# First cross attention of a six-stage decoder: one element deeper in flight, keys masked on ScalarE

## The chip, the cores and the metric

The kernel runs on one core of one Trainium2 chip, as one launch. The metric is the device time of that core in microseconds (us); before the change it was 3356.13, the median of three runs from 3353.65 to 3359.01.

## What is computed

Two decoder layers over 64 elements of 128 tokens with 128 features, all in float32. Each of six parts adds its result to x and normalises: a gated linear attention, **a cross attention with 16 heads of 8 features**, a mixture of experts, a selective scan, a second cross attention with 16 heads of 64 features, and a feed-forward with ternary weights. The change touches the first cross attention alone:

```python
qh = (q @ Wq + bq).reshape(b, n, HEADS, DK).transpose(0, 2, 1, 3)      # b = 64, n = 128, HEADS = 16, DK = 8
kh = (k @ Wk + bk).reshape(b, -1, HEADS, DK).transpose(0, 2, 1, 3)     # k = v = ctx_1024, 77 rows
vh = (v @ Wv + bv).reshape(b, -1, HEADS, DK).transpose(0, 2, 1, 3)
scores = jnp.einsum('bhnd,bhmd->bhnm', qh * scale, kh)
scores = scores + attn_bias[:, None, :, :] + attention_mask[:, None, :, :]
probs = jax.nn.softmax(scores, axis=-1)
ctx = jnp.einsum('bhnm,bhmd->bhnd', probs, vh)
ctx = ctx.transpose(0, 2, 1, 3).reshape(b, n, HEADS * DK)
return ctx @ Wo + bo
```

Around it stands `x = _layernorm(x + _L0_xattn_ref(x, ctx_1024, ctx_1024, fside_BxSxS2_0, mask_BxSxS2_ff0, ...))`.

## The kernel before

`build` (end of the file) runs the parts as phases one behind the other: `run_phase` calls the phase and then `finish_statistics`, and each phase opens and closes its semaphores with blocks of all engines. x stays in SBUF for the whole kernel. The first cross attention is `phase_cross0` (L574 to L918); its names begin with `b_`.

Its unit of work is one batch element `i` of 64. The 16 heads are four quads `r` of four heads `j`. A head has only 8 features, so four heads share a group of 32 rows of PE: `keys` (L778) writes the projected keys four times, each copy multiplied by `head_mask`, a mask with the softmax scale in it that leaves one head's 8 rows in every group of 32. `score` (L850) then needs four matmuls of 32 rows with 4 x 77 = 308 columns. `values` (L788) writes v four times in the same way, times `b_v_mask`, a mask of 77 x 512 that is loaded from memory, and `mix` (L876) multiplies the copy of head `j` with the transposed probabilities, four column groups at a time.

One element goes through these steps, each a small function of its engine's block, with a semaphore for each result:

- ACT `normalise` (L716, writes `b_xs`), PE `turn_x` (L836), ACT `copy_xT`, PE `project` (L842: q, k and v into one PSUM bank), ACT `copy_q`, DVE `keys`, DVE `values`, PE `score`;
- DVE `bias_max` (L794: adds the side input and takes the row maximum), POOL `lower` (L679: subtracts it), ACT `exp`, DVE `sums` (L806: sum and reciprocal), POOL `divide` (L685);
- PE `turn_p` and ACT `copy_p`, four times, once per `j`, with two PSUM banks in turn, PE `mix` behind each; ACT `copy_c`, PE `project_out` (L888), DVE `leave` (L812: adds to x and takes the statistics).

The order of the work is written out by hand: each engine has a function `step(i, s)` that says which stage of which element it does in step `i`, and the engines run their steps in order. In step `i` element `i` is turned and mixed, `bias_max`, `lower` and `exp` are done for element `i + 2`, `sums` and `divide` for `i + 1`, the scores on PE for `i + 3`, the projections, keys and values for `i + 4`, and ACT ends its step with `normalise(i + 5)`. Every buffer has four slots (`slots`, L579), so `values(i + 4)` has to wait for the last mix of element `i`. `turn_x` waits for `values` of the element ahead, since both use the bank `b_in_ps`. `around` (L645) writes the first ten and the last eight steps out and runs the 52 in between in a hardware loop, four steps a round:

```python
for i in range(-5, 5):
    step(i, i % slots)
with eng.Fori(5, B - 10, slots) as i:
    for k in range(slots):
        step(i + k, (1 + k) % slots)
for i in range(B - 7, B + 1):
    step(i, i % slots)
```

## Time and profile before

| what | us |
|---|---|
| median of three runs (lowest, highest) | 3356.13 (3353.65, 3359.01) |
| the profiled execution | 3354.66 |
| its span in the profile | 3352.8 |
| busy: PE, DVE, POOL, ACT | 2726.7, 2409.3, 2033.2, 1716.0 |
| first row of the phase on ACT, last on DVE | 184.26, 651.24 |

All other tables and rows of this document are from that one execution. Times in a timeline count from the span's start. The phase of the change lies between 184 and 651 us. `PE` is the matmul engine, `PEld` its loading of weights, `DVE` the vector engine, `ACT` the scalar engine, `POOL` GpSimd, `SP` the engine that starts the DMAs; L747 is line 747 of the kernel. A float32 matmul is recorded as two or more instructions. Matmuls overlap, so from one to the next it is the starts that count, and the same holds for instructions of ACT and DVE that follow without a wait.

### The profile page before, as it was taken

How to read it: one execution, taken by the hardware profiler on the slowest of the kernel's cores; microseconds unless marked ns; L12 is line 12 of the kernel's file. 1: busy time of each engine (PE TensorE's matmuls, PEld its weight loads, DVE VectorE, ACT ScalarE, POOL GpSimd, SP SyncE). 2: the span in 40 equal slices, each digit the busy share in tenths (PEclk: the TensorE clock that was granted, in tenths of full speed). 3: DMA queues.
4: the chain of work that ended last, by engine and by line, in shares of the span. 5: the costliest groups of instructions: out<-in, count | busy, mean ns of one | idle time of the engine just before them, and what ended most of it. 6: DMA issues, size and time to landing. Idle time of an engine off the chain costs nothing. (4 is left out here: it accounts for less than half of the span.)

```text
span 3352.8 us, 51512 instructions
## 1 busy us (share of the span) xinstructions
PE 2726.7 (81%) x16584; PEld 1624.9 (48%) x16584; DVE 2409.3 (72%) x3855; ACT 1716.0 (51%) x3206; POOL 2033.2 (61%) x1795
## 2 busy tenths in 40 slices
PE   7868888799788817888798788868999999997555
PEld 5545555455455512333333333325777777775222
DVE  6968888655433344999989999885666666665777
ACT  7746666533222205656566665534444444443665
POOL 5447777556545546999989999862333333333444
PEclk9979999889899958899988998889999999998555
DMA  6810000011044433334333333310000000000000
GB/s 208 334 21 18 17 18 16 4 34 38 32 140 137 126 107 139 139 140 151 131 147 139 141 151 128 149 63 16 5 3 5 5 3 5 5 3 1 13 16 22
DMA packets 130121, 249.21 MB, mean 74 GB/s; under 512 B 41057, under 2 KB 97910, under 8 KB 109314
## 3 DMA queue, kind: packets, MB, share of 16 engines
q1 hardware_dynamic: 119250, 228.98, 19.9%
q0 software_dynamic: 9088, 16.94, 1.5%
q8 instruction: 107, 1.75, 0.2%
q10 hardware_dynamic: 1584, 0.79, 0.1%
q14 instruction: 92, 0.75, 0.1%
HBM read 189.34 MB, written 59.13 MB: 74 GB/s over the span
## 5 line engine op out<-in xcount | busy, mean ns | idle before, releaser
L1819 POOL TENSOR_TENSOR s_drive<-s_du,s_b_sb 128x1024 f32<-128x1024 f32 x256 | 599.0, 2354 | 35.3 <-DVE s_state_ps L2066 34.8
L2179 PE MATMUL s_y_ps<-s_read,w_ident 128*128 128x512 f32 x832 | 451.6, 673 | 163.2 <-DVE s_read L2079 163.0
L2066 DVE TENSOR_TENSOR_SCAN s_state_ps<-s_decay_ps,s_drive 128x512 f32<-128x512 f32 x416 | 486.6, 1215 | 98.0 <-ACT s_decay_ps L1965 87.0
L1965 ACT ACTIVATE s_decay_ps<-s_delta,neg_rate 128x508 f32<-128x508 f32 x512 | 346.4, 685 | 316.0 <-DVE s_state_ps L2066 266.0
L2179 PEld LDWEIGHTS s_y_ps<-s_read,w_ident 128*128 128x128 f32 x832 | 158.6, 204 | 426.6 <-DVE s_read L2079 266.2
L2417 ACT ACTIVATE c_pT<-c_turn_ps 77x512 f32<-77x512 f32 x256 | 149.1, 587 | 244.8 <-PE c_turn_ps L2618 244.5
L2079 DVE TENSOR_TENSOR s_read<-s_state_ps,s_c_sb 128x1024 f32<-128x1024 f32 x208 | 254.7, 1224 | 7.2
L2373 POOL TENSOR_TENSOR c_p<-c_p,c_norm 128x1232 f32<-128x1232 f32 x64 | 143.8, 2247 | 156.5 <-DVE c_norm L2498 156.5
L1422 POOL DMA_INDIRECT m_y_scratch<-e_y,e_index x156 | 152.6, 978 | 134.5 <-DVE e_index L1456 59.9
L2351 POOL TENSOR_TENSOR x<-c_xs,w_c_bo 128x128 f32<-128x128 f32 x64 | 30.8, 482 | 304.6 <-DVE c_xs L2458 304.6
L747 ACT ACTIVATE b_pT<-b_turn_ps 77x512 f32<-77x512 f32 x256 | 145.5, 591 | 120.1 <-PE b_turn_ps L872 120.1
L681 POOL TENSOR_TENSOR b_p<-b_p,b_top 128x1232 f32<-128x1232 f32 x64 | 143.9, 2248 | 93.8 <-DVE b_top L804 93.8
L1046 POOL DMA_INDIRECT m_rows_scratch<-m_xs,m_index x128 | 126.2, 986 | 94.8 <-DVE m_xs L1174 54.7
L872 PE MATMUL b_turn_ps<-w_ident,b_p 128*77 128x128 f32 x1024 | 162.3, 293 | 15.2 <-POOL b_p L687 15.2
L687 POOL TENSOR_TENSOR b_p<-b_p,b_norm 128x1232 f32<-128x1232 f32 x64 | 143.9, 2248 | 29.4 <-DVE b_norm L810 29.3
L2618 PEld LDWEIGHTS c_turn_ps<-w_ident,c_p 128*77 128x77 f32 x1024 | 124.7, 150 | 73.2 <-issue 47.6
L2618 PE MATMUL c_turn_ps<-w_ident,c_p 128*77 128x128 f32 x1024 | 155.1, 280 | 4.5 <-POOL c_p L2373 3.5
L2475 DVE TENSOR_TENSOR c_v<-c_f_ps,w_c_bv 77x512 f32<-77x512 f32 x128 | 87.8, 686 | 95.9 <-PE c_f_ps L2588 95.9
L2425 ACT ACTIVATE c_oT<-c_f_ps 128x512 f32<-128x512 f32 x128 | 76.4, 597 | 152.2 <-PE c_f_ps L2636 152.2
L2480 DVE TENSOR_REDUCE c_top<-c_s_ps 128x16 f32<-128x1232 f32 x64 | 92.2, 1441 | 79.7 <-PE c_s_ps L2602 79.7
L2602 PEld LDWEIGHTS c_s_ps<-c_k,c_q 64*128 64x128 f32 x2048 | 119.3, 188 | 51.2 <-issue 51.2
L1441 ACT ACTIVATE e_silu<-e_g_ps 128x512 f32<-128x512 f32 x78 | 46.6, 598 | 190.6 <-PE e_u_ps L1497 155.5
(371 smaller groups left out, 6931.2 us busy)
## 6 DMA issues: line engine op xcount, KB each, us to landing
s_b_sb<-s_bc_scratch SPq DMA_DIRECT2D x64, 1024.0 KB, 4.7
s_c_sb<-s_bc_scratch SPq DMA_DIRECT2D x64, 1024.0 KB, 4.7
m_rows_scratch<-fill SPq DMA_DIRECT2D x33, 1040.0 KB, 27.5
e_w<-in_m_we_dram SPq DMA_DIRECT2D x39, 384.0 KB
e_xg<-m_rows_scratch SPq DMA_DIRECT2D x39, 260.0 KB
k_y<-m_y_scratch SPq DMA_DIRECT2D x32, 256.0 KB, 3.6
out_dram<-q_result SPq DMA_DIRECT2D x16, 256.0 KB, 2.3
x<-in_x_dram SPq DMA_DIRECT2D x13, 256.0 KB, 2.8
```

What stands on the lines that cost most here:

```text
L681: nc.gpsimd.tensor_tensor(p[:, s, :, :], p[:, s, :, :], top[:, s, :].unsqueeze(2).broadcast_to([128, heads, S2]), ALU.subtract).then_inc(l ...
L687: nc.gpsimd.tensor_tensor(p[:, s, :, :], p[:, s, :, :], norm[:, s, :].unsqueeze(2).broadcast_to([128, heads, S2]), ALU.mult).then_inc(p_no ...
L747: nc.scalar.activation(pT[:, j, :, :], turn_ps[0:S2, j % 2, :].rearrange("p (r t) -> p r t", t=128), ACT.Copy).then_inc(pT_ready.sem, 1)
L872: last = nc.tensor.transpose(turn_ps[0:S2, j % 2, r * 128:(r + 1) * 128], p[:, s, per * r + j, :], core.ident[:, :])
L1422: nc.gpsimd.indirect_dma_start(y_dram[:, :], bass.IndirectOffsetOnAxis(index[:, t % y_slots, j:j + 1], 0), y[:, t % y_slots, j, :], None, ...
L1819: nc.gpsimd.tensor_tensor(drive[:, (g * states + n) % drives, :, :], du[:, s, :, :], b_sb[:, n, :].unsqueeze(1).broadcast_to([128, halves, ...
L1965: nc.scalar.activation(decay[:, m, :, 1:], delta[:, s, m, :].rearrange("p (b t) -> p b t", t=T)[:, :, 1:], ACT.Exp, scale=core.neg_rate[:, ...
L2066: nc.vector.tensor_tensor_scan(home[:, h, :], decay[:, h, :, :].rearrange("p b t -> p (b t)"), drive[:, (g * states + n) % drives, h, :], ...
L2079: nc.vector.tensor_tensor(read[:, r % deep, :, :], state[:, :, :], c_sb[:, n // per_chunk % 2, n % per_chunk, :].unsqueeze(1).broadcast_to ...
L2179: last = nc.tensor.matmul(y_ps[:, m, :], core.ident[:, :], read[:, r % deep, m, :], start=False, stop=False)
L2417: nc.scalar.activation(pT[:, per * r:per * (r + 1), :], turn_ps[0:S2, r % 2, :].rearrange("p (j t) -> p j t", t=128), ACT.Copy).then_inc(p ...
L2618: last = nc.tensor.transpose(turn_ps[0:S2, r % 2, j * 128:(j + 1) * 128], p[:, i % 2, per * r + j, :], core.ident[:, :])
```

## The change

- Everything ahead of the turn of p is done one element earlier: projections, keys and values for element `i + 5` in step `i`, scores on PE for `i + 4`, `bias_max`, `lower` and `exp` for `i + 3`, `sums` and `divide` for `i + 2`. Buffers get five slots.
- `normalise(i + 6)` stands at the head of ACT's step, where `normalise(i + 5)` stood at its end.
- `keys` moves from DVE (one instruction for all four copies) to ACT (four activations of 128 x 77, one per copy, with the mask's column as scale and mask times bias, `b_k_bias`, as bias). It stands between the third and the last `copy_p`.
- `b_v_own` is a row of 4 x 128 columns per slot, set to zero once; `values` copies only the 128 projected columns into it, 8 at a time and 32 apart, with a jump to the next 128 for the next head, and `mix` reads 32 columns of which 8 are the head's. It has six slots, and `values` waits for the keys instead of the queries. `b_v_mask` is gone.
- The hardware loop is gone: all steps are written out.

```diff
--- before.py
+++ after.py
@@ -576,7 +576,7 @@
     x = core.x
     heads, dk, quads = 16, 8, 4
     per = heads // quads
-    slots = 4
+    slots, v_slots = 5, 6
     with ExitStack() as ctx:
         def sb(name, shape, dt=F32):
             return ctx.enter_context(nc.sbuf_tensor(name, shape, dt))
@@ -598,7 +598,8 @@
         xT = sb("b_xT", [128, slots, 128])
         qT = sb("b_qT", [128, slots, 128])
         k_own = sb("b_k_own", [128, slots, per, S2])
-        v_own = sb("b_v_own", [S2, slots, per, 128])
+        v_own = sb("b_v_own", [S2, v_slots, per * 128])
+        k_bias = sb("b_k_bias", [128, per])
         p = sb("b_p", [128, slots, heads, S2])
         pT = sb("b_pT", [S2, per, quads, 128])
         top = sb("b_top", [128, slots, heads])
@@ -614,7 +615,7 @@
         y_ps = s_ps[:, quads - 1, 384:512]
         scores = s_ps[:, :, 0:per * S2].rearrange("p r (j s) -> p r j s", s=S2)
 
-        prepared = sig("b_prepared")
+        prepared = sig("b_prepared", 3)
         loaded = sig("b_loaded", 48)
         side_ready = sig("b_side_ready")
         x_normed = sig("b_x_normed")
@@ -645,12 +646,7 @@
 
         def around(eng, step):
 
-            for i in range(-5, 5):
-                step(i, i % slots)
-            with eng.Fori(5, B - 10, slots) as i:
-                for k in range(slots):
-                    step(i + k, (1 + k) % slots)
-            for i in range(B - 7, B + 1):
+            for i in range(-6, B + 1):
                 step(i, i % slots)
 
         open_signals(nc, signals, [core.landed["b"]])
@@ -701,13 +697,13 @@
                                         core.w["b_bo"][:, :], ALU.add).then_inc(bo_added.sem, 1)
 
             def step(i, s):
+                if on(i, 3):
+                    lower(i + 3, (s + 3) % slots)
                 if on(i, 2):
-                    lower(i + 2, (s + 2) % slots)
-                if on(i, 1):
-                    divide(i + 1, (s + 1) % slots)
-                if on(i, 4):
-                    add_side(i + 4, s)
-                    add_bo(i + 4, s)
+                    divide(i + 2, (s + 2) % slots)
+                if on(i, 5):
+                    add_side(i + 5, s)
+                    add_bo(i + 5, s)
 
             around(pool, step)
 
@@ -736,6 +732,17 @@
                 nc.scalar.activation(qT[:, s, :], q_ps, ACT.Identity,
                                      bias=core.w["b_bq"][:, 0:1]).then_inc(q_ready.sem, 1)
 
+            def keys(i, s):
+
+                if i == 0:
+                    act.wait_ge(prepared.sem, prepared.at(0, 2))
+                if behind(i, slots):
+                    act.wait_ge(scored.sem, scored.at(i - slots, 1))
+                for j in range(per):
+                    last = nc.scalar.activation(k_own[:, s, j, :], k_ps, ACT.Identity, bias=k_bias[:, j:j + 1],
+                                                scale=core.w["head_mask"][:, j:j + 1])
+                last.then_inc(k_ready.sem, 1)
+
             def exp(i, s):
                 act.wait_ge(lowered.sem, lowered.at(i, 1))
                 nc.scalar.activation(p[:, s, :, :], p[:, s, :, :], ACT.Exp).then_inc(exped.sem, 1)
@@ -755,19 +762,21 @@
                                      bias=core.w["b_bv"][:, 0:1]).then_inc(cT_ready.sem, 1)
 
             def step(i, s):
-                if on(i, 4):
-                    copy_xT(i + 4, s)
+                if on(i, 6):
+                    normalise(i + 6, (s + 1) % slots)
+                if on(i, 5):
+                    copy_xT(i + 5, s)
                 for j in range(per):
                     if on(i, 0):
                         copy_p(i, s, j)
-                    if j == 1 and on(i, 4):
-                        copy_q(i + 4, s)
-                if on(i, 2):
-                    exp(i + 2, (s + 2) % slots)
+                    if j == 1 and on(i, 5):
+                        copy_q(i + 5, s)
+                    if j == 2 and on(i, 5):
+                        keys(i + 5, s)
+                if on(i, 3):
+                    exp(i + 3, (s + 3) % slots)
                 if on(i, 0):
                     copy_c(i, s)
-                if on(i, 5):
-                    normalise(i + 5, (s + 1) % slots)
 
             around(act, step)
 
@@ -775,21 +784,20 @@
         def _(dve):
             nc.vector.scalar_tensor_tensor(shift[:, :], core.mean[:, :], -1.0, core.rstd[:, :],
                                            ALU.mult, ALU.mult).then_inc(prepared.sem, 1)
-
-            def keys(i, s):
-                dve.wait_ge(q_ready.sem, q_ready.at(i, 1))
-                if behind(i, slots):
-                    dve.wait_ge(scored.sem, scored.at(i - slots, 1))
-                nc.vector.scalar_tensor_tensor(
-                    k_own[:, s, :, :], k_ps.unsqueeze(1).broadcast_to([128, per, S2]),
-                    core.w["b_bk"][:, :], core.w["head_mask"][:, :].unsqueeze(2).broadcast_to([128, per, S2]),
-                    ALU.add, ALU.mult).then_inc(k_ready.sem, 1)
+            nc.vector.tensor_tensor(k_bias[:, :], core.w["head_mask"][:, :],
+                                    core.w["b_bk"][:, 0:1].broadcast_to([128, per]),
+                                    ALU.mult).then_inc(prepared.sem, 1)
+            nc.vector.memset(v_own[:, :, :], 0.0).then_inc(prepared.sem, 1)
 
             def values(i, s):
-                if behind(i, slots):
-                    dve.wait_ge(mixed.sem, mixed.at(i - slots, per))
-                nc.vector.tensor_tensor(v_own[:, s, :, :], v_ps.unsqueeze(1).broadcast_to([S2, per, 128]),
-                                        core.w["b_v_mask"][0:S2, :, :], ALU.mult).then_inc(v_ready.sem, 1)
+                dve.wait_ge(k_ready.sem, k_ready.at(i, 1))
+                if i == 0:
+                    dve.wait_ge(prepared.sem, prepared.at(0, 3))
+                if behind(i, v_slots):
+                    dve.wait_ge(mixed.sem, mixed.at(i - v_slots, per))
+                own = v_own[:, i % v_slots, :].rearrange("p (j r c) -> p j r c", j=per, r=quads)[:, :, :, 0:dk]
+                nc.vector.tensor_copy(own, v_ps.rearrange("p (r j c) -> p j r c", r=quads, j=per)
+                                      ).then_inc(v_ready.sem, 1)
 
             def bias_max(i, s):
                 dve.wait_ge(scored.sem, scored.at(i, 1))
@@ -819,15 +827,14 @@
                                    here).then_inc(x_steps.sem, 1)
 
             def step(i, s):
-                if on(i, 2):
-                    bias_max(i + 2, (s + 2) % slots)
+                if on(i, 3):
+                    bias_max(i + 3, (s + 3) % slots)
                 if on(i, -1):
                     leave(i - 1, (s - 1) % slots)
-                if on(i, 1):
-                    sums(i + 1, (s + 1) % slots)
-                if on(i, 4):
-                    keys(i + 4, s)
-                    values(i + 4, s)
+                if on(i, 2):
+                    sums(i + 2, (s + 2) % slots)
+                if on(i, 5):
+                    values(i + 5, s)
 
             around(dve, step)
 
@@ -852,8 +859,8 @@
                 pe.wait_ge(k_ready.sem, k_ready.at(i, 1))
                 if behind(i, 1):
                     pe.wait_ge(biased.sem, biased.at(i - 1, 1))
-                if behind(i, 4):
-                    pe.wait_ge(x_steps.sem, x_steps.at(i - 4, 1))
+                if behind(i, 5):
+                    pe.wait_ge(x_steps.sem, x_steps.at(i - 5, 1))
                 for r in range(quads):
                     rows = slice(32 * r, 32 * r + 32)
                     last = nc.tensor.matmul(s_ps[:, r, 0:per * S2], qT[rows, s, :],
@@ -881,27 +888,28 @@
                 pe.wait_ge(pT_ready.sem, pT_ready.at(i, j + 1))
                 for r in range(quads):
                     cols = slice(32 * r, 32 * r + 32)
-                    last = nc.tensor.matmul(c_ps[cols, :], v_own[:, s, j, cols], pT[:, j, r, :],
+                    first = 32 * r + (128 - dk) * j
+                    last = nc.tensor.matmul(c_ps[cols, :], v_own[:, i % v_slots, first:first + 32], pT[:, j, r, :],
                                             start=(j == 0), stop=(j == per - 1))
                 last.then_inc(mixed.sem, 1)
 
             def project_out(i, s):
                 pe.wait_ge(cT_ready.sem, cT_ready.at(i, 1))
-                if on(i, 3):
-                    pe.wait_ge(biased.sem, biased.at(i + 3, 1))
+                if on(i, 4):
+                    pe.wait_ge(biased.sem, biased.at(i + 4, 1))
                 else:
                     pe.wait_ge(x_steps.sem, x_steps.at(i - 1, 1))
                 nc.tensor.matmul(y_ps, cT[:, s, :], core.w["b_wo"][:, :],
                                  start=True, stop=True).then_inc(y_ready.sem, 1)
 
             def step(i, s):
-                if on(i, 4):
-                    turn_x(i + 4, s)
+                if on(i, 5):
+                    turn_x(i + 5, s)
                 if on(i, 0):
                     turn_p(i, s, 0)
                     turn_p(i, s, 1)
-                if on(i, 4):
-                    project(i + 4, s)
+                if on(i, 5):
+                    project(i + 5, s)
                 if on(i, -1):
                     project_out(i - 1, (s - 1) % slots)
                 if on(i, 0):
@@ -909,8 +917,8 @@
                     turn_p(i, s, 2)
                     mix(i, s, 1)
                     turn_p(i, s, 3)
-                if on(i, 3):
-                    score(i + 3, (s + 3) % slots)
+                if on(i, 4):
+                    score(i + 4, (s + 4) % slots)
                 if on(i, 0):
                     mix(i, s, 2)
                     mix(i, s, 3)
@@ -3167,7 +3175,7 @@
 
 WEIGHTS = {
     "a": ["ident", "a_wqkvT", "upper", "a_wuvT", "a_woutT"],
-    "b": ["b_wq", "b_wk", "b_wv", "b_wo", "b_bq", "b_bk", "b_bv", "b_bo", "b_v_mask", "head_mask"],
+    "b": ["b_wq", "b_wk", "b_wv", "b_wo", "b_bq", "b_bk", "b_bv", "b_bo", "head_mask"],
     "m": ["m_router", "m_bias", "m_earlier", "m_w1", "m_w3", "m_w2", "m_ids", "m_region",
           "m_tile_of", "m_tile_end"],
     "s": ["s_bo", "s_b_in", "s_A_log", "s_conv_w", "s_taps", "s_conv_b", "s_D", "s_w_in",
@@ -3213,7 +3221,6 @@
         "b_bq": c(i["L0_xattn_bq"].reshape(128, 1)),
         "b_bk": c(i["L0_xattn_bk"].reshape(128, 1)),
         "b_bv": c(i["L0_xattn_bv"].reshape(128, 1)),
-        "b_v_mask": c(np.tile((np.arange(128) // 8 % 4 == np.arange(4)[:, None]).astype(np.float32), (128, 1, 1))),
         "b_bo": c(np.tile(i["L0_xattn_bo"], (128, 1))),
         "head_mask": head_mask,
 
```

ACT in one step, before (in the steps that are written out; `b_pT` is the copy of turned p, `b_p` exp, `b_cT` the copy of the mixed values):

```order
L722 ACTIVATE b_xs<-x,b_shift,rstd 128x128
L730 ACTIVATE b_xT<-b_in_ps 128x128
L747 ACTIVATE b_pT<-b_turn_ps 77x512 x2
L736 ACTIVATE b_qT<-b_in_ps,w_b_bq 128x128
L747 ACTIVATE b_pT<-b_turn_ps 77x512 x2
L741 ACTIVATE b_p<-b_p 128x1232
L754 ACTIVATE b_cT<-b_c_ps,w_b_bv 128x128
```

and after:

```order
L718 ACTIVATE b_xs<-x,b_shift,rstd 128x128
L726 ACTIVATE b_xT<-b_in_ps 128x128
L754 ACTIVATE b_pT<-b_turn_ps 77x512 x2
L732 ACTIVATE b_qT<-b_in_ps,w_b_bq 128x128
L754 ACTIVATE b_pT<-b_turn_ps 77x512
L742 ACTIVATE b_k_own<-b_in_ps,b_k_bias,w_head_mask 128x77 x4
L754 ACTIVATE b_pT<-b_turn_ps 77x512
L748 ACTIVATE b_p<-b_p 128x1232
L761 ACTIVATE b_cT<-b_c_ps,w_b_bv 128x128
```

The rows keep their order, but the first row now writes an element that PE turns a step later, and four activations stand ahead of the last `b_pT`.

DVE in one step, before (`b_p` is the addition of the side input, `b_top` the maximum, `x` and `stats` the element that leaves):

```order
L799 TENSOR_TENSOR b_p<-b_s_ps,b_side_sum 128x1232
L804 TENSOR_REDUCE b_top<-b_p 128x16
L816 TENSOR_TENSOR x<-b_s_ps,x 128x128
L818 BN_STATS stats<-x 128x6
L808 TENSOR_REDUCE b_norm<-b_p 128x16
L810 RECIPROCAL b_norm<-b_norm 128x16
L783 SCALAR_TENSOR_TENSOR b_k_own<-b_in_ps,w_b_bk,w_head_mask 128x308
L791 TENSOR_TENSOR b_v_own<-b_in_ps,w_b_v_mask 77x512
```

and after:

```order
L807 TENSOR_TENSOR b_p<-b_s_ps,b_side_sum 128x1232
L812 TENSOR_REDUCE b_top<-b_p 128x16
L824 TENSOR_TENSOR x<-b_s_ps,x 128x128
L826 BN_STATS stats<-x 128x6
L816 TENSOR_REDUCE b_norm<-b_p 128x16
L818 RECIPROCAL b_norm<-b_norm 128x16
L799 COPY b_v_own<-b_in_ps 77x16x8
```

The instruction for the keys is gone from DVE, and that for v has a quarter of the columns, in runs of 8.

## Rows read from the trace of the kernel before

**Rows 1.** Busy us (instructions) of each engine by stretch, granted PE clock, DMA
```profile
300.00:350.00 50.00, 40.35 (x489) 27.53 (x491) 44.72 (x60) 33.99 (x66) 37.93 (x30) 1.00 0.09 17
380.00:390.00 10.00, 8.79 (x89) 6.48 (x88) 7.67 (x10) 6.10 (x12) 5.44 (x6) 0.83 0.11 20
```

**Rows 2.** Waits of 210 to 610 us: total, times, longest
```profile
PE b_in_ps L840 <- ACT b_xs L722: 67.7, 57, 1.5
```

**Rows 3.** Order of time, one step: start us, us, engine, what [idle before]
```profile
307.95 0.59 ACT L747 ACTIVATE b_pT<-b_turn_ps 77x512 f32<-77x512 f32 x1 [0.35 <-PE b_turn_ps L872]
...
309.28 0.69 DVE L791 TENSOR_TENSOR b_v_own<-b_in_ps,w_b_v_mask 77x512 f32<-77x512 f32 x1 [0.31 <-PE b_c_ps L884]
309.56 0.35 ACT L754 ACTIVATE b_cT<-b_c_ps,w_b_bv 128x128 f32<-128x128 f32 x1
309.81 0.48 ACT L722 ACTIVATE b_xs<-x,b_shift,rstd 128x128 f32 x1
...
310.35 0.33 PE L840 MATMUL b_in_ps<-w_ident,b_xs 128*128 128x128 f32 x1 [1.14 <-ACT b_xs L722]
310.72 0.28 ACT L730 ACTIVATE b_xT<-b_in_ps 128x128 f32<-128x128 f32 x1 [0.42 <-PE b_in_ps L840]
...
310.90 1.10 PE L872 MATMUL b_turn_ps<-w_ident,b_p 128*77 128x128 f32 x8 [0.22 <-POOL b_p L687]
...
311.84 0.39 PE L845 MATMUL b_in_ps<-b_xT,w_b_wq 128*128 128x128 f32 x2
...
312.46 0.39 PE L894 MATMUL b_s_ps<-w_b_wo,b_cT 128*128 128x128 f32 x2
...
312.78 0.43 PE L884 MATMUL b_c_ps<-b_pT,b_v_own 77*32 77x128 f32 x8
...
313.14 0.66 PE L872 MATMUL b_turn_ps<-w_ident,b_p 128*77 128x128 f32 x4
...
313.83 0.59 ACT L747 ACTIVATE b_pT<-b_turn_ps 77x512 f32<-77x512 f32 x1 [0.80 <-PE b_turn_ps L872]
...
314.08 0.66 PE L872 MATMUL b_turn_ps<-w_ident,b_p 128*77 128x128 f32 x4
...
314.78 0.59 ACT L747 ACTIVATE b_pT<-b_turn_ps 77x512 f32<-77x512 f32 x1 [0.35 <-PE b_turn_ps L872]
...
315.27 0.53 DVE L783 SCALAR_TENSOR_TENSOR b_k_own<-b_in_ps,w_b_bk,w_head_mask 128x308 f32<-128x308 f32 x1
315.28 1.22 ACT L741 ACTIVATE b_p<-b_p 128x1232 f32<-128x1232 f32 x1
```

**Rows 4.** Order of time on ACT: four activations in a row, two places
```profile
28.64 1.15 ACT L355 ACTIVATE a_w_kv<-a_k_ps,a_k_ms 128x128 f32<-128x128 f32 x4 [1.66 <-POOL a_k_ms L291]
29.89 0.37 ACT L364 ACTIVATE a_th_q<-a_q_ps,a_q_ms 128x128 f32<-128x128 f32 x1
...
658.48 1.65 ACT L1075 ACTIVATE m_xs<-x,m_shift,rstd 128x128 f32<-128x128 f32 x4 [3.56 <-DVE m_shift L1250]
```

**Rows 5.** Order of time, PE's turns of x in the fill
```profile
190.35 0.45 PE L840 MATMUL b_in_ps<-w_ident,b_xs 128*128 128x128 f32 x1 [1.72 <-DVE b_v_own L791]
...
201.15 0.47 PE L840 MATMUL b_in_ps<-w_ident,b_xs 128*128 128x128 f32 x1 [2.98 <-ACT b_xs L722]
...
205.51 0.47 PE L840 MATMUL b_in_ps<-w_ident,b_xs 128*128 128x128 f32 x1 [0.62 <-ACT b_xs L722]
```

**Rows 6.** Order of time: first turns of p of steps 1, 59, 60; the end
```profile
213.89 1.04 PE L872 MATMUL b_turn_ps<-w_ident,b_p 128*77 128x128 f32 x8
...
617.63 1.10 PE L872 MATMUL b_turn_ps<-w_ident,b_p 128*77 128x128 f32 x8
...
624.25 1.10 PE L872 MATMUL b_turn_ps<-w_ident,b_p 128*77 128x128 f32 x8 [1.47 <-POOL b_p L687]
...
627.68 0.59 ACT L747 ACTIVATE b_pT<-b_turn_ps 77x512 f32<-77x512 f32 x1 [0.35 <-PE b_turn_ps L872]
...
650.95 0.29 DVE L818 BATCH_NORM_STATS2 stats<-x 128x6 f32<-128x128 f32 x1
```

## The prediction

> **What bounds the kernel now.** The phases of this kernel follow one another behind barriers, so only the first cross attention matters: what it gains or loses is the whole effect. I read its stretch in four views. First the busy time by stretch [rows 1]: in 50 us PE is busy 40.35, DVE 44.72, POOL 37.93, ACT 33.99. No engine is full, so a chain of hand-overs sets the pace. Then the waits [rows 2]: PE waits 67.7 us in 57 steps (1.2 us each) at the turn of x for `b_xs`, which ACT writes. Then the order of time [rows 3], where the reader is to follow one lap. From one last copy of p to the next (307.95, one period before 314.78) it is 6.83 us: the copy 0.50, exp 1.12, copy of c 0.25, normalise 0.54 until PE turns x, 0.55 until PE turns p (0.22 of it waiting for POOL's division), 0.94 for two turns of p, 0.62 projections, 0.32 output projection, 0.36 mix, 0.59 turn, 0.35 mix, 0.70 until ACT can copy. Sum 6.84. So the lap goes through ACT and PE in turn, each idle while the other works. DVE stands 0.31 us in this step at `b_v_own` for the last mix, so it has little slack; `values` waits for the mix of its own step.
>
> **What the change does to the lap.** Call t the start of ACT's last copy of p in one step.
>
> *Normalise* goes to the head of ACT's step and one element further ahead, so PE's turn of x waits for nothing: at t+0.65 (copy 0.59, hop 0.06, as 310.29 to 310.35) PE does the last mix, at about t+1.0 it turns x. *POOL's division* is now a whole step ahead of the turn of p, so its 0.22 goes too. But ACT still has, in this order, the copy 0.50, exp 1.12, copy of c 0.25, normalise 0.39 [rows 3, 4], (1.65-0.48)/3, and only then the copy of xT, at t+2.26. PE needs that xT for the projections, and they start at t+2.60 (0.28 and a hop of 0.06). PE alone would be there at about t+2.3 (0.33 for x, 0.94 for p). Then 0.62, 0.32, 0.36 to the third turn at t+3.90, 0.69 to ACT's third copy at t+4.59, its 0.50, and now the new work: four activations for the keys, K. They stand ahead of the last copy, so the lap closes at **P = 5.09 + K**.
>
> *K.* The trace has no 128x77 activation from PSUM with both a scale and a bias column. Nearest above: four from SBUF with both, 128 wide, start 0.39 us apart [rows 4]. Nearest below: four from PSUM with the scale column alone, 128 wide, start (1.15-0.37)/3 = 0.26 apart (0.37 is the length of a single one like them) [rows 4]. The slope over width: 0.59 for 512 columns against 0.28 for 128 [rows 3] is 0.8 ns a column, so 51 fewer save 0.04. That makes 0.35 and 0.22 each, K between 0.88 and 1.40. I take 0.32, nearer the upper row because it has both columns, less 0.03 for PSUM: K = 1.27 and **P = 6.36**. If they don't overlap at all each costs 0.41 to 0.48 and K is up to 1.94.
>
> The Trainium skill (ScalarE: Activation LUTs, "What ACT_TABLE_LOAD costs") prices an activation at 186 ns plus 0.833 ns a column, 93 ns for each pointer operand, and an overlap of 93 ns back to back; its estimate for K would be 1.37, the lap 6.46 and the result about 6 us later than mine. The starts 0.39 apart above agree with it to 0.01.
>
> *Other engines in 6.36 us.* One step's busy time is 6.84/50 of the stretch [rows 1]. DVE: 6.12, less the keys 0.53 and v's 0.69, plus a copy of 128 columns, 0.3 by my choice, between a quarter of v's 0.69 for four times the columns and, if the runs of 8 cost something, the whole of it: 5.2, at most 5.6. The new copy waits for the keys, hence for ACT, and the bias of the next element stands behind it on DVE. From the output projection to the end of the reciprocal it takes 2.81 (312.46 to 315.27) [rows 3]; PE is there at t+3.22, so DVE is free for the copy at t+6.03, and the keys are ready at about t+6.46. PE's next turn of x waits for that copy, but PE comes 1 us after the keys and the copy takes 0.3. POOL: 5.19. PE: 5.52. The six v slots free a value long before it is wanted, so DVE's 0.31 goes. None of them closes a longer lap; the tightest is DVE, which would bind at about 5.93.
>
> *The hardware loop is gone*; 52 steps that ran in 13 rounds are written out. Between the first turn of p of step 1 (213.89) and of step 59 (617.63) lie 58 steps in 403.7 us [rows 6], 6.96 each, not 6.84: 7 us go at the loop's jumps and in stretches such as 380 to 390, where the granted clock is 0.83 [rows 1], a mean over 2.4 and 1.2 GHz. What PE does ahead of such a fall is what it does in every step: it stands idle 1.2 us before turning x [rows 2]. That gap closes, the longest left is some 0.6 us ahead of the last mix, so I take these 7 us as gone: 58 x (6.96-6.36) = **34.8 us saved**. If they stay, 7 less.
>
> *Fill.* One element more goes in ahead of the first turn of p. Two rounds took 10.8 us and the last 4.4 (190.35, 201.15, 205.51) [rows 5]. The added round has a bias and maximum, a sum over exp, and keys on the ACT-PE lap of the fill: **5.7 us lost**, bounds 4.4 and 9. The memset of v (3072 columns; at the 0.69 us per 512 of v's row at most 4.1 us) starts with the phase (its first ACT row is at 184.26), and element 1's turn of x, which waits for values, was at 190.35 [rows 5]: hidden; if not, 1 us. The bias of the keys is one small DVE instruction. SP's loads run one element further ahead, and a step has three small ones: nothing.
>
> *Drain.* From step 59 on there are no keys and no projections. Before it took 33.6 us (617.63 to 651.24) [rows 6], because the last elements waited for POOL's divisions (1.47 at 624.25). Now POOL is a step ahead: a step is 3.43 (624.25 to 627.68) plus 0.65 and 0.36, so 4.44; four of them 17.8, 1.4 for the last elements' lowering and exp, 6.2 from the last turn to the end (3.43, 0.65 and four short hand-overs): 25.4. **8.2 us saved**, bounds 4 and 9.
>
> The mask of v is no longer loaded (one of the early weight DMAs): nothing, since phase a does not wait for it.
>
> **Sum**: -34.8 + 5.7 - 8.2 = -37.3. The profiled execution took 3354.66 (span 3352.8), so 3317.4; the median of the three runs, 3356.13, lies 1.5 above it: **3319 us**.
>
> **The rivals.**
> 1. *K smaller, then DVE binds.* With K at 0.88 P would be 5.97, close to DVE's own 5.93, and 22.6 us more are saved: 3294 to 3296. For: the scale-only row. Against: the two columns each cost something in every pair of rows. 5%.
> 2. *A middling lap*, 6.5 to 6.85: K at 1.4 and more, the clock stretches stay, or a hop that my lap leaves out. Each 0.1 us costs 5.8 us: 3327 to 3347. For: the lap has eleven links, most of them start to start in a loop where other work may have covered a hop. 21%.
> 3. *The four activations lose their overlap*, 0.48 each: P = 7.03, +4.1, fill +9.1 (five rounds of keys), drain -8.2: +5, 3361, within 0.2%, which is about what a measurement of this kernel can tell from no change. 5%.
> 4. *The slow side*: at the same place, between ACT's third and fourth copy, each of the four waits for the one ahead to end and a hop of 0.06: K = 4 x 0.54 = 2.18, P = 7.27, 58 x 0.31 = +18.0, fill +10.2, drain -8.2: +20, 3376. It turns slower than before (by over 0.2%) from K about 2.0. For: one DVE instruction of 0.53 becomes four of ACT, on the engine whose order closes the lap. Against: both rows of four in [rows 4] overlap. 7%. The Trainium skill (ScalarE: Activation LUTs, "Rules for kernel authors") says to put additions and multiplications on VectorE, not ScalarE; by that rule this side would be the likely one. The trace doesn't bear it out as long as DVE and not ACT has the fuller row.
> 5. *The change doesn't do what it says*: the deeper order fills no gap since the lap was another. Against: the 6.83 adds up link by link. In 3's price.
>
> The rest, 62%, is the forecast, with its own range 3305 to 3327.
>
> **How the numbers follow.** Faster by over 0.2% (6.7 us): forecast, rivals 1 and 2: 0.88. Within: 0.05. Slower: 0.07. The range runs from K = 0.88 with the full fill and a little less, 3298, to the middling lap with the clock stretches kept, 3342; outside it I leave some of rival 1, the end of 2, and 3 and 4: two in ten.
>
> **What would show it.** A step of 6.3 to 6.5 us in DVE's or PE's rows; four key activations starting 0.3 apart; no wait of PE for `b_xs` at the turn of x, instead about 0.6 ahead of the last mix for the copy of p and some 0.3 for xT; ACT waiting some 0.9 for PE once, at the third copy, and hardly at the first; DVE waiting about 0.5 for the keys; the first turn of p near 211.5; the end of the phase near 614. I am wrong if the keys start over 0.45 apart, if DVE has no wait left while the step is over 6.5, or if PE shows waits at the first turn of p.

## The result, and the profile after

| | before | after |
|---|---|---|
| median, us | 3354.89 (3348.59 to 3359.01, 4 runs) | 3311.62 (3309.53 to 3313.66, 4 runs) |
| ratio | | 0.9863, 95% interval 0.9849 to 0.9877 |
| profiled execution, span | 3354.66, 3352.8 | 3309.53, 3307.5 |
| first cross attention | 474.3 | 435.0 |
| mean granted clock | 0.897 | 0.903 |

The changed kernel is faster by 1.4%, 43 us; 3319 was predicted, and the range was 3298 to 3342. The length of a phase is here the time from its first statistics row to the next phase's (L140 in both kernels):

| us | scan | first cross attention | experts | Mamba | second cross attention | quantised rest |
|---|---|---|---|---|---|---|
| before | 179.1 | 474.3 | 594.2 | 1012.4 | 828.0 | 264.8 |
| after | 179.0 | 435.0 | 600.0 | 1005.0 | 825.7 | 262.8 |

So 39.2 of the 45.3 us of span lie in the phase that was changed, and 6.1 (+5.8 -7.4 -2.3 -2.0, and -0.2 of the scan) in phases that have the same instructions in both kernels. These phases move by as much between the runs below (the Mamba phase from 998 to 1011), so I read the 6.1 as spread.

The same stretches as [rows 1], the busy time of each engine, after:

```profile
300.00:350.00 50.00, 44.35 (x512) 29.38 (x512) 41.62 (x56) 43.48 (x102) 40.92 (x32) 1.00 0.11 21
380.00:390.00 10.00, 8.94 (x111) 5.57 (x108) 8.27 (x13) 8.47 (x20) 8.37 (x6) 1.00 0.09 18
```

ACT went from 33.99 to 43.48 in 50 us and DVE from 44.72 to 41.62 while the steps became denser; the granted clock between 380 and 390 is 1.00 where it was 0.83.

The waits of 220 to 580 us, after (total, times, longest):

```profile
ACT b_pT L754 <- PE b_turn_ps L879: 45.7, 57, 0.8
...
DVE b_v_own L799 <- ACT b_k_own L742: 31.1, 57, 0.5
DVE x L824 <- PE b_s_ps L902: 26.7, 57, 0.5
...
PE b_in_ps L852 <- ACT b_xT L726: 20.1, 56, 0.4
PE b_c_ps L892 <- ACT b_pT L754: 19.5, 56, 0.3
```

The 67.7 us of [rows 2] (210 to 610 us) are gone. PE now waits 0.35 a step for the copy of p ahead of the last mix and 0.36 for xT; ACT waits 0.80 once, at the third copy. The prediction had expected the first of these at some 0.6.

The order of time of one step, after (start us, us, engine, what [idle before]), beside [rows 3]:

```profile
306.09 0.60 ACT L754 ACTIVATE b_pT<-b_turn_ps 77x512 f32<-77x512 f32 x1
...
306.57 1.24 ACT L748 ACTIVATE b_p<-b_p 128x1232 f32<-128x1232 f32 x1
...
307.09 0.33 PE L847 MATMUL b_in_ps<-w_ident,b_xs 128*128 128x128 f32 x1
...
307.69 0.37 ACT L761 ACTIVATE b_cT<-b_c_ps,w_b_bv 128x128 f32<-128x128 f32 x1
...
307.94 0.50 ACT L718 ACTIVATE b_xs<-x,b_shift,rstd 128x128 f32<-128x128 f32 x1
...
308.32 0.28 ACT L726 ACTIVATE b_xT<-b_in_ps 128x128 f32<-128x128 f32 x1
...
308.65 0.49 PE L852 MATMUL b_in_ps<-b_xT,w_b_wq 128*128 128x128 f32 x2 [0.36 <-ACT b_xT L726]
...
309.38 0.39 PE L902 MATMUL b_s_ps<-w_b_wo,b_cT 128*128 128x128 f32 x2
...
309.70 0.43 PE L892 MATMUL b_c_ps<-b_pT,b_v_own 77*32 77x128 f32 x8
...
310.05 0.66 PE L879 MATMUL b_turn_ps<-w_ident,b_p 128*77 128x128 f32 x4
...
310.75 0.59 ACT L754 ACTIVATE b_pT<-b_turn_ps 77x512 f32<-77x512 f32 x1 [0.80 <-PE b_turn_ps L879]
...
311.25 1.31 ACT L742 ACTIVATE b_k_own<-b_in_ps,b_k_bias,w_head_mask 128x77 f32<-128x77 f32 x4
...
312.45 0.60 ACT L754 ACTIVATE b_pT<-b_turn_ps 77x512 f32<-77x512 f32 x1
312.59 0.29 DVE L799 COPY b_v_own<-b_in_ps 77x128 f32<-77x128 f32 x1 [0.55 <-ACT b_k_own L742]
```

From 306.09 to 312.45 it is 6.36 us, along the predicted lap: copy 0.48, exp 1.12, copy of c 0.25, normalise 0.38, copy of xT and hop 0.33, projections 0.73, output projection 0.32, mix 0.35, turn 0.70, third copy 0.50, keys 1.20. PE turns x at 307.09 and waits for nothing there. All steps but those of fill and drain take 6.35 to 6.37.

The two ends, PE's first turns of p of elements 0, 1 and 59, beside [rows 6], and the last element's statistics:

```profile
211.03 1.91 PE L879 MATMUL b_turn_ps<-w_ident,b_p 128*77 128x128 f32 x8
...
218.21 1.04 PE L879 MATMUL b_turn_ps<-w_ident,b_p 128*77 128x128 f32 x8
...
586.58 1.10 PE L879 MATMUL b_turn_ps<-w_ident,b_p 128*77 128x128 f32 x8
...
611.61 0.29 DVE L826 BATCH_NORM_STATS2 stats<-x 128x6 f32<-128x128 f32 x1
```

### The profile page after: what moved, and what is told of

Its sections match the earlier page's. It is cut to its first block and busy times, and to the rows that moved or that the text cites. A ratio compares the mean times of both kernels' runs of the same rounds, so it can differ in the third digit from the quotient of the medians.

```text
span 3307.5 us, 50313 instructions
## 1 busy us (share of the span) xinstructions
PE 2713.4 (82%) x16569; PEld 1613.3 (49%) x16584; DVE 2357.3 (71%) x3793; ACT 1772.6 (54%) x3462; POOL 2035.7 (62%) x1795
## 5 line engine op out<-in xcount | busy, mean ns | idle before, releaser
L879 PE MATMUL b_turn_ps<-w_ident,b_p 128*77 128x128 f32 x1024 | 152.3, 282 | 0.0
```

Source lines behind the costliest of these rows:

```text
L879: last = nc.tensor.transpose(turn_ps[0:S2, j % 2, r * 128:(r + 1) * 128], p[:, s, per * r + j, :], core.ident[:, :])
```

## Experiments

The runs have two levels of total time. The kernel before, measured again beside each group of experiments, has a median of 3275 to 3282 us beside experiments 1 to 6 and 10, and of 3356 (as above) beside 7 to 9. The difference is in the expert phase, 520 to 525 us in the first group and 594 to 600 in the second, whatever the first cross attention is; no run here shows what sets the level. Totals are therefore compared only as a ratio to the kernel before of the same group, and phases directly, by the same rows as above. "Step" is the distance of DVE's statistics rows of two elements.

| | step, us | phase, us | ratio to before, 95% interval |
|---|---|---|---|
| before | 6.84, 6.93 at loop jumps | 474.3 | |
| after | 6.36 | 435.0 | 0.9863 (0.9849 to 0.9877) |
| 1 before, written out | 6.64, 6.66 | 465.7 | 0.9970 (0.9957 to 0.9984) |
| 2 after, normalise last | 7.13 | 501.4 | 1.0064 (1.0040 to 1.0087) |
| 3 after, five v slots | 6.37 | 444.4 | 0.9884 (0.9866 to 0.9902) |
| 4 after, keys earlier | 5.61 | 391.0 | 0.9726 (0.9705 to 0.9748) |
| 5 after, keys on DVE | 5.67 | 393.7 | 0.9749 (0.9733 to 0.9766) |
| 6 after, two of four keys | 5.75 | 400.4 | 0.9760 (0.9725 to 0.9796) |
| 7 after, again | 6.36 | 438.0 | 0.9885 (0.9858 to 0.9912) |
| 8 after, masked v | 6.36 | 436.5 | 0.9867 (0.9839 to 0.9895) |
| 9 keys earlier, masked v | 5.61 | 393.1 | 0.9737 (0.9710 to 0.9764) |
| 10 as 3, again | 6.37 | 440.7 | 0.9895 (0.9860 to 0.9930) |

### 1. The kernel before, written out

```
-            for i in range(-5, 5):
-                step(i, i % slots)
-            with eng.Fori(5, B - 10, slots) as i:
-                for k in range(slots):
-                    step(i + k, (1 + k) % slots)
-            for i in range(B - 7, B + 1):
+            for i in range(-5, B + 1):
                 step(i, i % slots)
```

> The kernel before with its 52 looped steps written out and nothing else changed. Lap theory (the step is the chain through ACT and PE): only register work and the jumps go; the steps that were already written out took 6.6 to 6.7 us against 6.84 in the loop, so 52 x 0.17 + 1 = 10 us less, up to 15 with fewer low-clock stretches: 3341 to 3346. Rival (the loop was what cost, all else is decoration): most of the 43 us, below 3325.

The phase is 8.6 us shorter, as expected. The whole step is shorter, 6.64 to 6.66 against 6.84, not only the one at the jump. The turn of x is followed by that of p after 0.31 instead of 0.55. But POOL's division still releases the turn of p, 0.05 us after its end in every step at full clock (298.41 + 2.25, then 300.71):

```profile
298.41 2.25 POOL L682 TENSOR_TENSOR b_p<-b_p,b_norm 128x1232 f32<-128x1232 f32 x1
...
300.40 0.33 PE L835 MATMUL b_in_ps<-w_ident,b_xs 128*128 128x128 f32 x1 [1.24 <-ACT b_xs L717]
...
300.71 0.87 PEld L867 LDWEIGHTS b_turn_ps<-w_ident,b_p 128*77 128x77 f32 x8 [0.17 <-POOL b_p L682]
300.71 1.10 PE L867 MATMUL b_turn_ps<-w_ident,b_p 128*77 128x128 f32 x8
```

The low-clock stretches stay, at six places (steps of 8.05 to 8.19). PE's waits of 220 to 600 us in this kernel:

```profile
PE b_in_ps L835 <- ACT b_xs L717: 66.2, 55, 1.5
```

The 1.2 us gap of each step is as in [rows 2]; writing the loop out does not close it.

### 2. Normalise at the end of ACT's step again

```
-                if on(i, 6):
-                    normalise(i + 6, (s + 1) % slots)
                 if on(i, 5):
                     copy_xT(i + 5, s)
...
                 if on(i, 0):
                     copy_c(i, s)
+                if on(i, 6):
+                    normalise(i + 6, (s + 1) % slots)
```

> The changed kernel with normalise back at the end of ACT's step (still one element deeper). Lap theory: PE's turn of x waits again for exp, copy of c and normalise: 0.50+1.12+0.25+0.54+0.33+0.94+0.62+0.32+0.36+0.69+0.50+1.27 = 7.44 us a step, 58 x 1.08 = 63 us more than the changed kernel, about 3373, slower than the kernel before. Rival (the gain is DVE's lighter load): DVE's work is the same, so within 5 us of 3311.

All else of the change kept, this is 66.4 us more in the phase, and slower than before. The step at full clock is 7.13, less than expected. The expectation had added the keys' time in full to the old lap. In experiment 1 the third and fourth copies of p are 0.95 apart, because ACT waits for PE; with the keys between them they are 1.69 apart here (254.91 and 256.60), so only 0.74 of the keys is added. Between the copies of xT and of p it is 0.44 here and 0.64 in experiment 1. At least 0.14 of that is the deeper order: the turn of p follows that of x after 0.17, since POOL's division ends 0.64 before it (256.28 + 2.25, then 259.17). So 6.65 becomes 7.19, near the 7.13. The step explains 45 of the 66 us; 3 more are in the start (first element after 45.3 us instead of 42.1), and the rest is the clock: two steps in every five or six take 7.7 to 8.0, and two steps 9.3. PE's gap is back (220 to 600 us, and one step):

```profile
PE b_in_ps L847 <- ACT b_xs L718: 67.7, 51, 1.3
```

```profile
259.00 0.33 PE L847 MATMUL b_in_ps<-w_ident,b_xs 128*128 128x128 f32 x1 [1.33 <-ACT b_xs L718]
259.17 1.04 PE L879 MATMUL b_turn_ps<-w_ident,b_p 128*77 128x128 f32 x8
```

So the place of `normalise` at the head of the step is what pays for the change: 0.77 us a step and the low-clock stretches. The deeper order alone, at the old place of `normalise`, saves 0.14 to 0.20. No run has `normalise` at the head with the old depth, so whether the gain needs the extra element, and the fifth slots with it, stays open.

### 3. and 10. Five slots for v

```
-    slots, v_slots = 5, 6
+    slots, v_slots = 5, 5
```

> The changed kernel with five slots for v instead of six, so that values waits for the last mix of its own step again. Lap theory: the copy of v comes at t+1.15 instead of t+0.14, PE's turn of x at t+1.5 instead of t+1.0, the projections 0.18 later: step 6.54, 10 us more, about 3321. Rival (the sixth slot is idle reserve): no difference.

The total agreed with the expectation and its mechanism did not. The step is 6.37, so the sixth slot is worth 0.01 a step. DVE does wait for PE's last mix again, and PE, at its turn of x, for DVE (240 to 590 us):

```profile
DVE b_v_own L799 <- PE b_c_ps L892: 61.5, 55, 1.5
...
PE b_in_ps L847 <- DVE b_v_own L799: 31.7, 55, 0.9
```

but those 0.57 us of PE only take the place of the 0.36 for xT, which ACT would not have ready earlier. The 9.4 us are in the start: the first element leaves 45.9 us after the phase's start (42.1 in the changed kernel), the next after 9.67. These are the 10 us stretches from 214 and from 224 of experiment 3:

```profile
214.00:224.00 10.00, 9.43 (x67) 6.46 (x67) 4.56 (x5) 6.08 (x14) 5.59 (x6) 0.50 0.11 20
224.00:234.00 10.00, 9.43 (x67) 6.55 (x66) 5.24 (x7) 5.99 (x13) 5.18 (x5) 0.50 0.07 13
```

and the one from 214 of the changed kernel:

```profile
214.00:224.00 10.00, 8.99 (x107) 5.39 (x105) 6.75 (x11) 8.21 (x21) 8.07 (x6) 0.98 0.13 25
```

The granted clock stayed at 0.50 (1.2 GHz) twenty us longer. Whether the slot causes that was the question of experiment 10, the same kernel again:

> The kernel with five slots for v once more, since its 9.4 us lay in the start of the phase (granted clock 0.50 up to 234) and not in the steps of 6.37. If the fifth slot's wait keeps the clock down, the phase is again some 9 us longer than with six (444 against 435 to 438), with a first step near 9.7. If the clock's rise is a matter of chance, as the repeat of the changed kernel (438.0 against 435.0, the same steps) suggests, the phase is 436 to 440 and the first step 6.4 to 7.2.

This time the phase is 440.7 and the first step 6.87. The granted clock is 0.58 from 214 to 224 and 1.00 behind, so at least 3.7 of the 9.4 us were chance in when the clock rises. What is left can be set against experiment 7, where the clock rises at the same point: 0.52 and 0.58 in that stretch put the rise some 44.5 us after the phase's start in both. The phases are 438.0 and 440.7. The first elements are 1.0 us later with five slots, the steps take 0.01 more, two of them stumble for 0.5 together, and the last elements ahead of the drain keep to 6.37 where they take 5.98 and 5.80 with six. So the sixth slot is worth some 2.8 us, from one pair of runs. Whether it also lets the clock rise earlier stays open: in the changed kernel and its variants the rise is 34 to 44 us after the start with six slots, 45 and 55 us with five.

### 4. The keys ahead of the third copy of p

```
                     if j == 1 and on(i, 5):
                         copy_q(i + 5, s)
-                    if j == 2 and on(i, 5):
                         keys(i + 5, s)
```

> The changed kernel with the four activations for the keys one place earlier, ahead of ACT's third copy of p, where ACT waits 0.80 us a step for PE. Lap theory: K then fills that wait, the fourth copy starts about 5.5 us after the last one's, and ACT (5.43 start to start) and PE (5.49) set the step: 5.5 to 5.6, 58 x 0.8 = 46 us less, about 3265. Rival (the third copy is what PE waits for, so delaying it costs what it saves): within 5 us of 3311.

This moves no work to another engine and removes none: it puts the four activations where ACT would wait 0.80 for PE. 44.0 us less in the phase, step 5.61. ACT, DVE and PE in one step of it:

```profile
303.79 0.37 ACT L732 ACTIVATE b_qT<-b_in_ps,w_b_bq 128x128 f32<-128x128 f32 x1
...
304.05 1.33 ACT L742 ACTIVATE b_k_own<-b_in_ps,b_k_bias,w_head_mask 128x77 f32<-128x77 f32 x4
...
305.25 1.25 ACT L754 ACTIVATE b_pT<-b_turn_ps 77x512 f32<-77x512 f32 x2
...
306.17 0.22 DVE L798 COPY b_v_own<-b_in_ps 77x128 f32<-77x128 f32 x1
...
306.40 1.22 ACT L748 ACTIVATE b_p<-b_p 128x1232 f32<-128x1232 f32 x1
...
306.67 1.44 DVE L806 TENSOR_TENSOR b_p<-b_s_ps,b_side_sum 128x1232 f32<-128x1232 f32 x1 [0.27 <-PE b_s_ps L865]
307.10 0.33 PE L846 MATMUL b_in_ps<-w_ident,b_xs 128*128 128x128 f32 x1
```

No row of ACT has an idle time before it: ACT's own row of work, 5.61 from start to start, is now the bound, and the lap through PE fits in it. It is faster than both kernels, by 2.7% against before.

### 5. The keys on DVE

```
+            def keys(i, s):
+                dve.wait_ge(q_ready.sem, q_ready.at(i, 1))
...
+                nc.vector.scalar_tensor_tensor(
+                    k_own[:, s, :, :], k_ps.unsqueeze(1).broadcast_to([128, per, S2]),
+                    core.w["b_bk"][:, :], core.w["head_mask"][:, :].unsqueeze(2).broadcast_to([128, per, S2]),
+                    ALU.add, ALU.mult).then_inc(k_ready.sem, 1)
```

> The changed kernel with the keys back on DVE as one instruction (0.45 us when written out), all else as changed. Lap theory: ACT's lap loses K, the fourth copy can follow the third after 0.95, 5.54 a step; DVE's own row of work, 1.46+1.46+0.33+0.21+1.45+0.19+0.45+0.21 = 5.76, sets the step: 58 x 0.6 = 35 us less than the changed kernel, about 3277, and moving the keys to ACT was a loss inside the gain. Rival (relief of DVE is the gain): back towards the old step, over 3330.

The function goes from ACT to DVE, ahead of `values`. Step 5.67, phase 41.3 us shorter than the changed kernel's. DVE in one step of it:

```profile
304.33 0.25 DVE L814 RECIPROCAL b_norm<-b_norm 128x16 f32<-128x16 f32 x1
304.50 0.45 DVE L783 SCALAR_TENSOR_TENSOR b_k_own<-b_in_ps,w_b_bk,w_head_mask 128x308 f32<-128x308 f32 x1
304.99 0.29 DVE L795 COPY b_v_own<-b_in_ps 77x128 f32<-77x128 f32 x1
305.20 1.43 DVE L803 TENSOR_TENSOR b_p<-b_s_ps,b_side_sum 128x1232 f32<-128x1232 f32 x1
```

DVE has no idle time in the step: here it is the bound. Moving the keys to ACT, at the place where the change puts them, is thus a loss of 0.7 us a step inside a change that gains.

### 6. Two of the four key activations

```
-                for j in range(per):
+                for j in range(2):
                     last = nc.scalar.activation(k_own[:, s, j, :], k_ps, ACT.Identity, bias=k_bias[:, j:j + 1],
```

> The changed kernel with two of the four activations for the keys; the other two copies stay zero (set once), so half of the heads get scores of the side input alone. Halves K and nothing else. Lap theory: step 6.36 - 0.64 = 5.73, 58 x 0.63 = 37 us less, about 3274. The prediction's other bound: DVE closes at 5.93, 25 us less, about 3286; the step in the trace tells them apart. Rival (ACT's activations are beside the path): within 5 us of 3311.

The two copies left out are zero, so half of the heads miss their scores. Step 5.75: each activation left out takes 0.30 off the step. The lap holds 0.2 below the 5.93 at which the prediction let DVE bind.

### 7. The changed kernel again

> The changed kernel unaltered, beside two variants on the same chip. Two other things are open: whether its lap is the same on this chip, and whether the rest of the program, which took 5.9 us less in the first profile after, really changed. Theory (only the first cross attention changed; the rest differs from run to run): phase 435 us, steps of 6.36, and a ratio to before of 1 - 39/3280 = 0.988. Rival (the smaller instruction stream or the missing mask helps elsewhere too): a ratio of 0.986 as on the first chip, and s and m phases shorter than in the other experiments by some us each.

The ratio, 0.9885, is the theory's; its interval holds the rival's 0.986 too. The steps are the same to 0.01. The phase is 438.0, and the 3 us more lie in the start again: granted clock 0.52 from 214 to 224 against 0.98, first element after 45.1 us instead of 42.1. The Mamba phase took 1006.9 (before 1012.4, experiment 3 1011.1, experiment 6 998.4), the expert phase 597.4 (before 594.2). Nothing there follows the change.

### 8. and 9. v by the mask, as before

```
-                nc.vector.tensor_copy(own, v_ps.rearrange("p (r j c) -> p j r c", r=quads, j=per)
-                                      ).then_inc(v_ready.sem, 1)
+                nc.vector.tensor_tensor(v_own[:, i % v_slots, :].rearrange("p (j c) -> p j c", j=per),
+                                        v_ps.unsqueeze(1).broadcast_to([S2, per, 128]),
+                                        core.w["b_v_mask"][0:S2, :, :], ALU.mult).then_inc(v_ready.sem, 1)
...
-                    first = 32 * r + (128 - dk) * j
+                    first = 32 * r + 128 * j
```

> The changed kernel with the values as before: one multiplication by the mask over 512 columns (0.69 us) in the place of the copy of 128 (0.29), six slots, all else changed. Theory (the lap is ACT's and PE's, and DVE has 0.47 us of waiting for PE later in the step and 0.55 ahead of the values): the multiplication ends 0.4 later, just ahead of PE's turn of x, and the bias behind it eats DVE's later wait: step 6.36 to 6.40, phase 435 to 438, so the own columns of v are worth nothing at this place. Rival (DVE's work counts one for one): step 6.76, phase 458.

> The version with the keys ahead of the third copy of p (step 5.61, phase 391), and again the masked values of 512 columns. There DVE waits only 0.27 us in a step, for the scores. Theory: 0.4 more of DVE's work finds little to hide in; the values start when DVE comes, 0.2 to 0.3 ahead of PE's turn of x, which then waits, and the bias is later by 0.15 at least: step 5.75 to 5.85, phase 399 to 405. Rival (ACT's 5.43 and PE's 5.49 set the step, DVE doesn't): 5.61 to 5.65, phase 391 to 393.

Experiment 9 has the edit of experiment 4 as well. In neither does v as own columns gain anything: 6.36 and 5.61, the same steps. The values' row and their wait in experiment 8 (220 to 560 us):

```profile
L798 DVE TENSOR_TENSOR b_v_own<-b_in_ps,w_b_v_mask 77x512 f32<-77x512 f32 x53 | 36.4, 687 | 29.0 <-ACT b_k_own L742 29.0
```

against the changed kernel's (220 to 580 us):

```profile
L799 DVE COPY b_v_own<-b_in_ps 77x128 f32<-77x128 f32 x57 | 16.4, 287 | 31.1 <-ACT b_k_own L742 31.1
```

In the changed kernel that is 0.40 us less work a step, all of it behind a wait and ahead of another. For experiment 9 I had expected 5.75 to 5.85; the step stayed at the rival's 5.61. Behind another instruction the masked values take 0.54 from start to start, where the copy and the wait of 0.27 behind it take 0.50 (306.17 to 306.67 in experiment 4):

```profile
302.55 0.62 DVE L797 TENSOR_TENSOR b_v_own<-b_in_ps,w_b_v_mask 77x512 f32<-77x512 f32 x1
303.09 1.42 DVE L806 TENSOR_TENSOR b_p<-b_s_ps,b_side_sum 128x1232 f32<-128x1232 f32 x1
```

So the wait takes nearly all of it. DVE has no idle time left in this step, and neither has ACT: once more is taken off ACT, the narrower copy may be worth something, which no run here tries.

## Why the prediction was right, and where not

| | predicted | measured |
|---|---|---|
| 58 steps | -34.8 (6.36 each) | -35.4 (6.351) |
| fill | +5.7 | +4.5 |
| drain | -8.2 | -8.3 |
| first cross attention | -37.3 | -39.2 |
| the rest of the program | 0 | -6.1 |

The measured steps are (617.63 - 213.89) - (586.58 - 218.21); the fill is from the phase's first DVE row to element 1's turn of p, the drain from element 59's to the end of the last statistics.

**The lap held.** P = 5.09 + K came out as 5.16 + 1.20. Experiments 2, 4 and 6 change one link each and the step follows: the gap back, the keys in an idle slot, half of K away. The links without K, which rival 2 doubted, were right to 0.07 together, but not one by one: the projections take 0.73 (308.65 to 309.38) where the prediction put the 0.62 of a lap in which PE reached them without a wait; the others are off by 0.02 at most, most of them shorter.

**K** was taken as 1.27 from two rows of [rows 4] and is 1.20: the starts are 0.30 apart, each takes 0.41, between the two bounds 0.22 and 0.35. An estimate from the figures of the Trainium skill (ScalarE: Activation LUTs, "What ACT_TABLE_LOAD costs") is 0.436 for one and, with its overlap, 0.34 a start, so 1.37; the measured 0.409 and 0.30 are lower. The error of 0.07 in K and that in the other links cancel, so that the lap came out as 6.36 to the hundredth is luck.

**The fill** was 1.2 us shorter than said; the memset (2.62 us, from 184.72) ended 2.8 us ahead of the first values, so it was hidden. In the repeat the start was 3 us longer. The fill's size depends on when the clock rises, a term that the prediction did not have; its bounds of 4.4 and 9 cover both.

**The drain** is right in sum. POOL is ahead, as said, but the first three of its steps took 4.80, 4.92 and 5.03 instead of 4.44, and the surplus is the 1.4 us that had been set aside for the last elements' exp.

**The loop.** The 7 us above 58 x 6.84 went. 13 jumps at 0.09 are 1.2 of them and the low-clock stretches the rest. Those stay in experiment 1, where only the loop goes, and are gone where the gap closes, as the prediction argued. What it did not have is the loop's other cost, 0.2 in every step, which was hidden in the 6.84 it started from. Of the 0.55 between the turns of x and p, 0.24 went with the loop (experiment 1) and 0.14 with POOL's earlier division (experiment 2), where the prediction had put 0.22 on the division.

**Wrong: DVE "would bind at about 5.93".** Its work, 5.2 us a step, was right, the place was not. The step compared when DVE comes to the values with when the keys are ready; what counts is PE's next turn of x, and in experiment 4 DVE copies at 306.17 and PE turns x at 307.10. DVE binds only by its own row of work, 5.67 with the keys in it (experiment 5). The 3294 of rival 1, which rests on it, was thus no floor. The forecast used the bound only to say that it does not bind at 6.36.

**Not asked: is ACT the right place?** The slow side (rival 4) did not come, because four activations overlap at 0.30 apart. But the prediction weighed only whether the keys on ACT would eat the gain and did not price the kernel without that part. Experiment 5 does: 5.67 against 6.36. The Trainium skill (ScalarE: Activation LUTs, "Rules for kernel authors") would leave additions and multiplications to VectorE. At the change's place it is borne out; experiment 4 shows that it is the place, not the engine, that costs: in ACT's idle slot the same four give 5.61.

**The rest of the program** was assumed fixed and took 6.1 less in the profiled run, which is most of the difference between 3319 and 3311.6. In the ten more profiles no phase follows the change: without the first cross attention the span is 2793.8 in experiment 1 and 2785 to 2801 in experiments 2 to 6 and 10. So this is spread, argued from the ranges and not shown by itself.

## What to carry to other kernels

Where two engines wait for one another in turn, follow one lap from start to start and ask of each piece of work whether it lies on it: the same four activations cost 1.20 us in the lap and next to nothing in the 0.80 us where their engine waits. Price each part of a change against the version without it: this one gained by the place of one instruction, by 0.2 a step in the written-out loop and by up to 0.2 in POOL's earlier division, lost 0.7 us a step by the place of the keys, and got nothing from 0.40 us less work on an engine that waited on both sides. A total that comes out as expected proves no mechanism: in experiment 3 it did, and the time was somewhere else.

## What the runs showed of the hardware

- The granted clock falls in kernels in which PE stands idle 1.2 to 1.3 us once a step: at five places in the kernel before, six in experiment 1, every five or six steps in experiment 2. In the changed kernel and experiments 3 to 10, where PE's longest wait of the step is 0.57, every 10 us stretch from 240 to 540 has 1.00.
- The clock's rise at the phase's start is not fixed: with the same instructions it was 0.98 or 0.52 from 214 to 224 us, and 3 us of the phase hang on it. In the kernel before it was 0.71 already from 204 to 214.
- A copy of 128 columns in runs of 8 takes 0.29 us (0.22 behind another instruction, experiment 4), as much as an addition of 128 contiguous ones on DVE (L824, 0.29). No run has the same copy in one piece. A memset of 3072 columns takes 2.62 us, 0.85 ns a column.
- The masked multiplication for the keys takes 0.45 us behind another instruction in steps that are written out (experiments 1 and 5), 0.53 at the same place in the loop, and 0.54 behind a wait in the fill of experiment 1.
- The expert phase takes 594 to 600 us in five profiles and 520 to 525 in seven, with the same instructions; no run here tried why.
